# Low parts of the decay matrices on a second engine, and another bank order for the first FFN products

## The chip, the cores and the metric

The kernel runs on one core of a Trainium2 chip. Its metric is the device time of one execution in microseconds. A core has five engines with a program each: TensorE (PE), VectorE (DVE), ScalarE (ACT), GpSimd (POOL) and SyncE (SP), which here only issues DMAs. Each engine works through its program in order. They meet at semaphores: an instruction waits until a count is reached and raises another when it is done.

## The reference

```python
xn = layernorm(x)                                    # x: 2 x 2048 x 512
# one Mamba2 layer
x_branch, z = split(xn @ in_proj_w.T)                # 1024 columns each
x_branch = silu(causal_conv4(x_branch) + conv_b)
X, dt, B, C = split(x_branch @ x_proj_w.T)           # 16 heads of 64, state 128
dt = softplus(dt @ dt_proj_w.T + dt_proj_b);  A = -exp(A_log) * dt
L = exp(segsum(A))                                   # decay inside a chunk, lower triangle
Y = (C B^T * L) @ (X * dt) + C @ state * exp(cumsum(A))
Y = (Y + D * X) * silu(z);   attn = Y @ out_proj_w.T
# one ternary FFN
h = sigmoid(xn @ q(w1).T) * (xn @ q(w2).T);   ffn = h @ q(w3).T   # q: to -1, 0, 1
out = x + attn + ffn                                 # hidden size 1408
```

## The kernel before

The 4096 tokens are worked through in 8 blocks of 512 (256 of either sequence). A float32 operand is carried as two float16 tiles, a high part (a rounded copy) and a low part (what the rounding left), and a product is three matmuls: high by high, low by high, high by low.

One block has these stages. The branch products and the convolution come first (`x_branch`), then the projections to B, C and dt. Then come eight units u = 0..7, each one chunk of 128 tokens and one half of the heads. A unit holds:

- the decay matrices, in two groups g = 0, 1 of four heads (`decay`): ACT takes the differences of the running sums (L985) and their exponential (L990) into `edc[g]`, DVE multiplies by `gt`, the masked product of B and C (L1365), ACT writes the high part (L997) and DVE the low part (L1371) into one of four `mdc` tiles;
- the projection of X (PE L613), its copy to `xs` on ACT (L949), times dt on DVE (`xdt`, L1315), its high part on ACT (L955) and low part on DVE (L1319); POOL makes `xst` and the skip term from them (L1688, L1691);
- `scan`: PE multiplies decay matrices and `xdt` parts (L645, after a wait for `m_lo` and `xdt_lo`), DVE adds and gates (L1407, L1410); POOL adds the skip term to y before that (L1709);
- the state's update, the gate (`project_z`, PE L523, ACT L936, DVE L1262) and, for an earlier unit, the output projection (PE L696, from block 1 on) with its sum on DVE (L1433).

The decay matrices of unit u+1 are made while PE works on unit u. Then the FFN follows: 11 pairs of up products (PE L723, ACT L1032, DVE L1444) and the down products (L741), with the next block's branch products between them. The loops over blocks and units, written out for each engine, set the order of all instructions. A buffer or PSUM bank is taken again only after a wait for its last reader.

In block 0 the kernel also makes the ternary weights. Their thresholds come from sums over each matrix: PE adds them up in one column of bank 3 (L775), DVE turns this into bounds (L1466 to L1472), POOL compares (L1720) and DVE finishes the tile (L1487). Up product m, half j, goes to a bank that `up_bank` names:

```python
return banks[2 * ((m + 1) % 2) + j]
```

So up product 0 fills banks 2 and 3, and its second half, in bank 3, waits in block 0 until the third matrix's sum has been read there (`bounds` at 7). After up product 0 PE turns the last unit's y (L670, `turn_first(7)`), and after up product 1 it does the last output projection of block 0 (L680), which waits for the low part of that y (`yt_lo`, DVE L1421).

Of the kernel before, what the change touches and what calls it, by code (L numbers as in the profile page):

```python
# [8 lines left out]
ACT = mybir.ActivationFunctionType  # L9
# [5 lines left out]
P = 128  # L15
# [57 lines left out]
def mamba_ffn_block(nc, x, w_in, conv_w, conv_b, w_x, w_xdt, w_dt, dt_bias, a_log, d_skip, w_out,  # L73
# [48 lines left out]
    with ctx:  # L122
# [179 lines left out]
        def sync_program(sp):  # L302
# [12 lines left out]
            def load_prep(kind, n):  # L315
# [3 lines left out]
                if kind == "tern" and n >= n_early:  # L319
# [3 lines left out]
                    elif use >= 2:  # L323
                        sp.wait_ge(S["m_lo"], at(0, "m_lo", 12 + use))
# [145 lines left out]
        def tensor_program(pe):  # L470
# [163 lines left out]
            def scan(b, u):  # L634
# [4 lines left out]
                for g in range(2):  # L639
                    pe.wait_ge(S["m_lo"], at(b, "m_lo", 2 * u + g))  # L640
# [59 lines left out]
            def ffn_up(b, m):  # L700
                for j in range(2):
# [139 lines left out]
        def scalar_program(act):  # L841
# [11 lines left out]
            def x_branch(b, m):  # L853
# [119 lines left out]
            def decay(b, u):  # L973
                c, hf = units[u]
                for g in range(2):
# [3 lines left out]
                    if u:  # L979
                        act.wait_ge(S["m_lo"], at(b, "m_lo", 2 * (u - 1) + g))  # L980
# [10 lines left out]
                for g in range(2):  # L991
# [5 lines left out]
                    act.mul(mdc[2 * (u % 2) + g][:, 0, :], edc[g][:], M_SCALE / B_SCALE ** 2).then_inc(S["m_hi"], 1)  # L997
# [28 lines left out]
            def ffn_up(b, m):  # L1026
# [5 lines left out]
                act.activation(tnh[m % 2][:], up_bank(m, 0)[:], ACT.Tanh,  # L1032
# [129 lines left out]
        def vector_program(dve):  # L1162
# [196 lines left out]
            def decay(b, u):  # L1359
# [77 lines left out]
            def ffn_up(b, m):  # L1437
                dve.wait_ge(S["up_tanh"], at(b, "up_tanh", m))
                dve.wait_ge(S["up_mm"], at(b, "up_mm", 2 * m + 1))
                if b == 0 and m < 2:  # L1440
# [4 lines left out]
                                         in1=up_bank(m, 1)[:], op0=ALU.add,  # L1445
# [78 lines left out]
            for b in range(nb):  # L1524
# [33 lines left out]
                dve.tensor_tensor(gt[:], by_head(banks[3][:], P),  # L1558
# [257 lines left out]
```

## Time and profile before

| what | value |
|---|---|
| time, median of 3 runs | 1618.42 us (1616.63 to 1618.63) |
| the profiled execution's own time | 1617.01 us |
| its span, first to last instruction | 1615.2 us |
| PE busy | 1559.1 us, 97% |
| DVE, ACT, POOL busy | 1203.7, 886.9, 495.6 us |
| mean granted TensorE clock | 0.989 |

The span lies 1.8 us under the execution's own time, which holds the start and the end around it. Busy times of different engines overlap. PE's busy share is drawn with modelled ends of matmuls, so a short wait can hide under the end of the matmul before it. The DVE, ACT and POOL shares say how much they work, and not whether anyone waits for them.

### The profile page before, as it was taken

The page shows a single profiled execution, that of the slowest core. Times are in us where ns is not written, and L with a number is a line of the kernel's source. Part 1 is how long each engine was busy: PE and PEld are TensorE (multiplying, and loading weights), DVE is VectorE, ACT ScalarE, POOL GpSimd, SP SyncE. Part 2 cuts the span into 40 slices and gives each one's busy share as a digit, 9 for nine tenths or more (in the row PEclk, how much of TensorE's full clock was granted, in tenths as well). Part 3 has the DMA queues.
Part 4 walks back from the last instruction along what each step waited for, and adds up shares of the span by engine and source line. Part 5 has one row for each costly group of instructions (what it writes and reads, how often), then busy time and mean ns, then how long its engine had stood idle before and what let it go on. Part 6 is the DMA issues. An engine that isn't in the chain of part 4 may idle for free.

```text
span 1615.2 us, 25318 instructions
## 1 busy us (share of the span) xinstructions
PE 1559.1 (97%) x9086; PEld 744.3 (46%) x9086; DVE 1203.7 (75%) x1876; ACT 886.9 (55%) x1840; POOL 495.6 (31%) x480
## 2 busy tenths in 40 slices
PE   7779899999999999999999999999999999999999
PEld 3334444544444444444444444444444544444444
DVE  7878776699566985689856897568966699576862
ACT  6687435565356644466454663646636565356641
POOL 3116664233033321234221431314303233033210
PEclk9799999999999999999999999999999999999999
DMA  7155430242402432133321333213350242402320
GB/s 266 55 168 175 140 105 14 62 104 74 89 27 68 99 97 56 37 86 85 85 53 47 81 97 92 26 60 89 84 103 14 66 106 71 87 27 73 97 67 26
DMA packets 228605, 131.66 MB, mean 82 GB/s; under 512 B 175200, under 2 KB 176992, under 8 KB 228480
## 3 DMA queue, kind: packets, MB, share of 16 engines
q1 hardware_dynamic: 228480, 130.05, 30.0%
q8 instruction: 72, 1.18, 0.3%
q14 instruction: 53, 0.43, 0.1%
HBM read 100.38 MB, written 29.62 MB: 80 GB/s over the span
## 4 chain that ended last, share of the span: by engine, by line
PE 62%; DVE 18%; issue 7%; ACT 5%; DMA 2%; POOL 2%; SPq 1%; DVEq 0%; POOLq 0%; ACTq 0%
PE bank L723 12%; PE bank L613 11%; PE bank L741 9%; PE bank L507 9%; PE bank L523 6%; PE bank L533 4%; DVE edc L1365 4%; PE bank L696 4%; DVE xst_lo L1336 2%; ACT edc L985 2%; PE bank L645 1%; DVE xin L1407 1%; DVE xdt L1315 1%; ACT mdc L997 1%; DVE xs L1414 1%
## 5 line engine op out<-in xcount | busy, mean ns | idle before, releaser
L613 PE MATMUL bank<-wx_hi,arena 128*128 128x512 f16 x1024 | 319.7, 382 | 0.0
L723 PE MATMUL bank<-xt_hi,q 128*128 128x512 f16 x704 | 267.0, 379 | 4.0 <-issue 4.0
L723 PE MATMUL bank<-xt_lo,q 128*128 128x512 f16 x704 | 267.0, 379 | 0.0
L1688 POOL TENSOR_TENSOR xst<-xdt,dst 128x512 f32<-128x512 f32 x60 | 62.6, 1043 | 490.3 <-DVE xdt L1315 490.3
L613 PE MATMUL bank<-wx_lo,arena 128*128 128x512 f16 x512 | 195.9, 383 | 0.0
L741 PE MATMUL bank<-q,arena 128*128 128x512 fp8e4 x704 | 163.3, 381 | 0.0
L985 ACT ACTIVATE edc<-csl,csv 128x128 f32<-128x128 f32 x512 | 155.8, 389 | 0.8 <-DMA csl<-sums 0.8
L1365 DVE TENSOR_TENSOR edc<-edc,gt 128x512 f32<-128x512 f32 x128 | 125.9, 1022 | 38.7 <-ACT edc L990 38.6
L613 PEld LDWEIGHTS bank<-wx_hi,arena 128*128 128x128 f16 x1024 | 101.1, 99 | 114.7 <-issue 3.7
L1024 ACT CAST arena<-full 128x512 f16<-128x512 f32 x88 | 54.2, 616 | 146.4 <-DVE full L1444 146.4
L1709 POOL TENSOR_TENSOR xin<-xin,xs 128x512 f32<-128x512 f32 x60 | 83.8, 1397 | 153.0 <-DVE xin L1388 153.0
L997 ACT ACTIVATE mdc<-edc 128x512 f16<-128x512 f32 x128 | 79.4, 630 | 61.5 <-DVE edc L1365 61.5
L723 PEld LDWEIGHTS bank<-xt_hi,q 128*128 128x128 fp8e4 x704 | 69.1, 98 | 87.7 <-issue 4.7
L741 PEld LDWEIGHTS bank<-q,arena 128*128 128x128 f16 x704 | 69.1, 98 | 83.6 <-issue 1.1
L723 PEld LDWEIGHTS bank<-xt_lo,q 128*128 128x128 fp8e4 x704 | 68.9, 98 | 82.8 <-issue 0.3
L955 ACT ACTIVATE xdt_hi<-xdt 128x512 f16<-128x512 f32 x64 | 40.3, 630 | 120.4 <-DVE xdt L1315 120.4
L507 PE MATMUL bank<-xt_hi,win_hi 128*128 128x512 f16 x256 | 97.0, 379 | 3.2 <-DVE win_lo L1229 2.5
L1691 POOL TENSOR_TENSOR xs<-xs,dsk 128x512 f32<-128x512 f32 x64 | 93.7, 1464 | 18.5 <-DVE xdt L1315 18.5
L1444 DVE SCALAR_TENSOR_TENSOR full<-tnh,bank 128x512 f32<-128x512 f32 x88 | 60.0, 682 | 52.0 <-PE bank L723 50.4
L523 PE MATMUL bank<-win_hi,xt_hi 128*128 128x512 f16 x256 | 97.1, 379 | 0.8 <-DVE xin L1262 0.7
L523 PE MATMUL bank<-win_lo,xt_hi 128*128 128x512 f16 x256 | 97.0, 379 | 0.0
L523 PE MATMUL bank<-win_hi,xt_lo 128*128 128x512 f16 x256 | 97.0, 379 | 0.0
(217 smaller groups left out, 3419.2 us busy)
## 6 DMA issues: line engine op xcount, KB each, us to landing
csl<-sums SPq DMA_DIRECT2D x128, 256.0 KB, 3.6
y_squares<-xs SPq DMA_DIRECT2D x56, 256.0 KB, 2.0
xin<-y_squares SPq DMA_DIRECT2D x168, 64.0 KB, 2.5
xin<-x SPq DMA_DIRECT2D x32, 256.0 KB, 4.0
res<-x SPq DMA_DIRECT2D x32, 256.0 KB, 3.4
out<-res SPq DMA_DIRECT2D x32, 256.0 KB, 2.0
raw<-w_ffn SPq DMA_DIRECT2D x25, 256.0 KB, 2.9
x_squares<-mdc SPq DMA_DIRECT2D x24, 256.0 KB, 2.0
```

Source lines behind the costliest of these rows:

```text
L507: i = pe.matmul(bk[:], wt[:, k, m * P:(m + 1) * P], act[:, k, :], start=(n == 1), stop=(n == 3 * kd))
L523: i = pe.matmul(banks[1][:], act[:, k, c * P:(c + 1) * P], wt[:, k, di + hf * half:di + (hf + 1) * half], start=(n == 1), stop=(n == 3 * kd))
L533: i = pe.matmul(bk[:], wt[:, k, col:col + ns], act[:, k, :], start=(n == 1), stop=(n == 3 * ki))
L613: i = pe.matmul(banks[0][:], act[:, k, c * P:(c + 1) * P], wt[:, k, hf * half:(hf + 1) * half], start=(n == 1), stop=(n == 3 * ki))
L696: i = pe.matmul(banks[7][:], act[:, k, :], wt[:, k, :], start=(hf == 0 and n == 1), stop=(hf == 1 and n == 3 * per))
L723: i = pe.matmul(up_bank(m, j)[:], q12[:, j, m, k, :], part[:, k, :], start=(n == 1), stop=(n == 2 * kd))
L741: i = pe.matmul(banks[c][:], hid[:, m, p, c * P:(c + 1) * P], q3[:, m, :], start=(m == p == 0), stop=(m == kf - 1 and p == 1))
L985: i = act.activation(edc[g][:, cols], csl[g][:, cols], ACT.Relu, scale=-1.0, bias=sml["csv"][:, c, h:h + 1])
L997: act.mul(mdc[2 * (u % 2) + g][:, 0, :], edc[g][:], M_SCALE / B_SCALE ** 2).then_inc(S["m_hi"], 1)
L1365: dve.tensor_tensor(by_head(edc[g][:], P), by_head(edc[g][:], P), gt[:, c, :].unsqueeze(1).to_broadcast([P, hpg, P]), ALU.mult).then_inc(S ...
L1691: pool.tensor_tensor(by_head(xs[u % 2][:], hd), by_head(xs[u % 2][:], hd), heads_over(dsk[:], hf * hph, hph, hd), ALU.mult).then_inc(S["sk ...
L1709: pool.tensor_tensor(yac[u % 2][:], yac[u % 2][:], xs[u % 2][:], ALU.add).then_inc(S["y_skip"], 1)
```

## The change

There are two parts. From block 1 on, POOL writes the low part of group g = 1 of each unit with a tensor_tensor, ahead of `project_x` in its program; DVE keeps group 0, and both groups in block 0. For that the scale (a power of two) moves from L997 and L1371 into `gt`, and the semaphore `m_lo` becomes `m_lo0` and `m_lo1`. In block 0 alone, up product m takes banks 0 and 1 for even m and 2 and 3 for odd m, the reverse of before; the waits on the banks go with them, and so do those of the down products.

```diff
-        def up_bank(m, j):
-            return banks[2 * ((m + 1) % 2) + j]
+        def up_bank(b, m, j):
+            return banks[2 * ((m + (b > 0)) % 2) + j]
...
-                    elif m == 0 and j == 0:
+                    elif m == (0 if b else 1) and j == 0:
                         pe.wait_ge(S["btok"], at(b, "btok", 0))
-                    elif m == 0:
+                    elif m == (0 if b else 1):
                         pe.wait_ge(S["gt"], at(b, "gt", 0))
                         if b == 0:
                             pe.wait_ge(S["bounds"], 7)
                     elif j == 0:
                         pe.wait_ge(S["xs"], at(b, "xs", 7))
...
+                        last = 9 + c // 2 if b else 10 - c // 2
                         if m == 0 and c % 2 == 0:
-                            pe.wait_ge(S["up_tanh"], at(b, "up_tanh", 9 + c // 2))
+                            pe.wait_ge(S["up_tanh"], at(b, "up_tanh", last))
...
-                    pe.wait_ge(S["m_lo"], at(b, "m_lo", 2 * u + g))
+                    pe.wait_ge(S[f"m_lo{g}"], at(b, f"m_lo{g}", u))
...
-                    act.mul(mdc[2 * (u % 2) + g][:, 0, :], edc[g][:], M_SCALE / B_SCALE ** 2).then_inc(S["m_hi"], 1)
+                    act.copy(mdc[2 * (u % 2) + g][:, 0, :], edc[g][:]).then_inc(S["m_hi"], 1)
...
-                for g in range(2):
+                for g in range(2 if b == 0 else 1):
                     md = mdc[2 * (u % 2) + g]
                     dve.wait_ge(S["m_hi"], at(b, "m_hi", 2 * u + g))
-                    dve.scalar_tensor_tensor(out=md[:, 1, :], in0=edc[g][:], scalar=M_SCALE / B_SCALE ** 2,
-                                             in1=md[:, 0, :], op0=ALU.mult,
-                                             op1=ALU.subtract).then_inc(S["m_lo"], 1)
+                    dve.scalar_tensor_tensor(out=md[:, 1, :], in0=edc[g][:], scalar=1.0, in1=md[:, 0, :],
+                                             op0=ALU.mult, op1=ALU.subtract).then_inc(S[f"m_lo{g}"], 1)
...
-                dve.tensor_tensor(gt[:], by_head(banks[3][:], P),
-                                  upp[:].unsqueeze(1).to_broadcast([P, chunks, P]),
-                                  ALU.mult).then_inc(S["gt"], 1)
+                dve.scalar_tensor_tensor(out=gt[:], in0=by_head(banks[3][:], P), scalar=M_SCALE / B_SCALE ** 2,
+                                         in1=upp[:].unsqueeze(1).to_broadcast([P, chunks, P]),
+                                         op0=ALU.mult, op1=ALU.mult).then_inc(S["gt"], 1)
...
+            def decay(b, u):
+                md = mdc[2 * (u % 2) + 1]
+                pool.wait_ge(S["m_hi"], at(b, "m_hi", 2 * u + 1))
+                pool.tensor_tensor(md[:, 1, :], edc[1][:], md[:, 0, :],
+                                   ALU.subtract).then_inc(S["m_lo1"], 1)
...
+                if b:
+                    decay(b, 0)
                 project_x(b, 0)
...
                     if u + 1 < len(units):
+                        if b:
+                            decay(b, u + 1)
                         project_x(b, u + 1)
```

On PE, between unit 7 of block 0 and its last output projection, the order was this (names in brackets are the semaphores waited for; `bank2` is PSUM bank 2, `q12` the ternary weights of the up products):

```order
L775 MATMUL bank3<-tsum,ones 128x1 [waits mag_sum,bounds,gt]
L723 MATMUL bank2<-xt_hi,q12 128x512 [waits tern_q,btok]
...
L723 MATMUL bank3<-xt_hi,q12 128x512 [waits tern_q,bounds,gt]
...
L670 MATMUL bank7<-idn,xin 128x128 [waits y_gated,yt_lo]
...
L723 MATMUL bank0<-xt_hi,q12 128x512 [waits tern_q,xs]
...
L723 MATMUL bank1<-xt_hi,q12 128x512 [waits tern_q,gate]
...
L680 MATMUL bank7<-wo_hi,yt_hi 128x512 [waits yt_lo]
```

In the changed kernel the same stretch of PE reads so:

```order
L778 MATMUL bank3<-tsum,ones 128x1 [waits mag_sum,bounds,gt]
L724 MATMUL bank0<-xt_hi,q12 128x512 [waits tern_q,xs]
...
L724 MATMUL bank1<-xt_hi,q12 128x512 [waits tern_q,gate]
...
L671 MATMUL bank7<-idn,xin 128x128 [waits y_gated,yt_lo]
...
L724 MATMUL bank2<-xt_hi,q12 128x512 [waits tern_q,btok]
...
L724 MATMUL bank3<-xt_hi,q12 128x512 [waits tern_q,bounds,gt]
...
L681 MATMUL bank7<-wo_hi,yt_hi 128x512 [waits yt_lo]
```

The wait for `bounds` has moved from the second to the fourth of these products, behind the transposes.

On DVE the units 0 and 1 of every block from 1 on began like this, from the first decay matrices on:

```order
L1365 TENSOR_TENSOR edc<-edc,gt 128x512 x2
L1371 SCALAR_TENSOR_TENSOR mdc<-edc,mdc 128x512 x2
L1315 TENSOR_TENSOR xdt<-xs,dt 128x512
L1319 SCALAR_TENSOR_TENSOR xdt_lo<-xdt,xdt_hi 128x512
L1336 SCALAR_TENSOR_TENSOR xst_lo<-xst,xst_hi 128x512
L1388 SCALAR_TENSOR_TENSOR xin<-bank,ecs 128x512
L1365 TENSOR_TENSOR edc<-edc,gt 128x512 x2
L1371 SCALAR_TENSOR_TENSOR mdc<-edc,mdc 128x512 x2
L1262 SCALAR_TENSOR_TENSOR xin<-tnh,bank 128x512
L1407 SCALAR_TENSOR_TENSOR xin<-bank,xin 128x512
L1410 TENSOR_TENSOR xin<-xin 128x512
L1315 TENSOR_TENSOR xdt<-xs,dt 128x512
```

In the changed kernel the same place on DVE is:

```order
L1368 TENSOR_TENSOR edc<-edc,gt 128x512 x2
L1375 SCALAR_TENSOR_TENSOR mdc<-edc,mdc 128x512
L1318 TENSOR_TENSOR xdt<-xs,dt 128x512
L1322 SCALAR_TENSOR_TENSOR xdt_lo<-xdt,xdt_hi 128x512
L1339 SCALAR_TENSOR_TENSOR xst_lo<-xst,xst_hi 128x512
L1391 SCALAR_TENSOR_TENSOR xin<-bank,ecs 128x512
L1368 TENSOR_TENSOR edc<-edc,gt 128x512 x2
L1375 SCALAR_TENSOR_TENSOR mdc<-edc,mdc 128x512
L1265 SCALAR_TENSOR_TENSOR xin<-tnh,bank 128x512
L1410 SCALAR_TENSOR_TENSOR xin<-bank,xin 128x512
L1413 TENSOR_TENSOR xin<-xin 128x512
L1318 TENSOR_TENSOR xdt<-xs,dt 128x512
```

One of each pair of low parts is gone. On POOL a unit of the changed kernel reads so, with the new instruction third:

```order
L1712 TENSOR_TENSOR state<-state,dec 128x512
L1719 TENSOR_TENSOR xin<-xin,xs 128x512
L1701 TENSOR_TENSOR mdc<-edc,mdc 128x512
L1691 TENSOR_TENSOR xst<-xdt,dst 128x512
L1694 TENSOR_TENSOR xs<-xs,dsk 128x512
```

It stands between the sum of y and the skip term and the product that makes `xst`; nothing else moved there.

## Rows read from the trace of the kernel before

**Rows 1.** The page: the span, and busy time by engine.
```profile
span 1615.2 us, 25318 instructions
PE 1559.1 (97%) x9086; PEld 744.3 (46%) x9086; DVE 1203.7 (75%) x1876; ACT 886.9 (55%) x1840; POOL 495.6 (31%) x480
```

**Rows 2.** Busy time by stage: window, length, then each engine, clock, DMA; block 4.
```profile
1019.00:1213.00 194.00, 192.29 (x1131) 91.19 (x1129) 146.97 (x230) 106.24 (x219) 56.17 (x57) 1.00 0.29 72
```

**Rows 3.** Whom PE waited for, whole run: us in total, times, longest.
```profile
PE bank L696 <- DVE res L1433: 6.1, 6, 1.6
PE bank L723 <- issue: 4.0, 1, 4.0
```

**Rows 4.** Timeline of block 0's FFN (start, us, engine, line); last row: the chain's.
```profile
188.95 0.38 PE L723 MATMUL bank<-xt_lo,q 128*128 128x512 f16 x1
193.04 0.15 DVE L1466 TENSOR_SCALAR gam<-bank 128x1 f32<-128x1 f32 x1
193.29 0.38 PE L723 MATMUL bank<-xt_hi,q 128*128 128x512 f16 x1 [3.96 <-issue]
193.36 0.74 DVE L1487 SCALAR_TENSOR_TENSOR q<-full,above,less 128x512 fp8e4<-128x512 f32 x1
198.91 0.38 PE L680 MATMUL bank<-wo_hi,yt_hi 128*128 128x512 f16 x1
207.81 0.69 DVE L1444 SCALAR_TENSOR_TENSOR full<-tnh,bank 128x512 f32<-128x512 f32 x1 [1.44 <-PE bank L723]
238.40 2.44 PE L486 MATMUL bank<-idn,xin 128*128 128x128 f32 x13 [2.09 <-DVE xin L1179]
...
405.40 13.81 PE bank L723 x64
```

**Rows 5.** Timeline of block 4, units 0 and 1.
```profile
1077.90 1.23 ACT L997 ACTIVATE mdc<-edc 128x512 f16<-128x512 f32 x2 [0.24 <-DVE edc L1365]
1078.56 1.29 DVE L1371 SCALAR_TENSOR_TENSOR mdc<-edc,mdc 128x512 f16<-128x512 f32 x2
1079.04 0.58 ACT L949 ACTIVATE xs<-bank 128x512 f32<-128x512 f32 x1
1079.77 0.68 DVE L1315 TENSOR_TENSOR xdt<-xs,dt 128x512 f32<-128x512 f32 x1
1080.54 1.04 POOL L1688 TENSOR_TENSOR xst<-xdt,dst 128x512 f32<-128x512 f32 x1 [30.83 <-DVE xdt L1315]
1081.15 0.97 DVE L1319 SCALAR_TENSOR_TENSOR xdt_lo<-xdt,xdt_hi 128x512 f16<-128x512 f32 x1 [0.70 <-ACT xdt_hi L955]
1082.18 0.20 PE L645 MATMUL bank<-xdt_hi,mdc 128*128 128x64 f16 x1
1087.43 0.58 ACT L936 ACTIVATE tnh<-bank 128x512 f32<-128x512 f32 x1
1088.16 0.68 DVE L1262 SCALAR_TENSOR_TENSOR xin<-tnh,bank 128x512 f32<-128x512 f32 x1
1088.90 0.39 PE L523 MATMUL bank<-win_hi,xt_hi 128*128 128x512 f16 x1
```

**Rows 6.** Timeline of block 4, decay of unit 7, and PE behind its scan.
```profile
1161.38 1.47 DVE L1371 SCALAR_TENSOR_TENSOR mdc<-edc,mdc 128x512 f16<-128x512 f32 x2
1161.49 0.63 ACT L997 ACTIVATE mdc<-edc 128x512 f16<-128x512 f32 x1 [1.05 <-DVE edc L1365]
1163.48 0.69 DVE L1410 TENSOR_TENSOR xin<-xin 128x512 f32<-128x512 f32 x1
1164.09 0.68 DVE L1315 TENSOR_TENSOR xdt<-xs,dt 128x512 f32<-128x512 f32 x1
1176.86 0.39 PE L696 MATMUL bank<-wo_hi,yt_hi 128*128 128x512 f16 x1 [0.91 <-DVE res L1433]
```

**Rows 7.** POOL forms: two in the timeline, one group (us busy, mean ns).
```profile
1109.10 1.27 POOL L1709 TENSOR_TENSOR xin<-xin,xs 128x512 f32<-128x512 f32 x1 [3.03 <-DVE xin L1388]
1159.26 1.65 POOL L1709 TENSOR_TENSOR xin<-xin,xs 128x512 f32<-128x512 f32 x1 [3.63 <-DVE xin L1388]
...
L1720 POOL TENSOR_SCALAR less<-raw,under 128x512 uint8<-128x512 f32 x14 | 25.4, 1820 | 8.0 <-DMA raw<-w_ffn 4.6 <-DVE q L1487 3.4
```

More of the change, by code:

```diff
@@ L42 @@
               "silu": 8, "s_lo": 8, "gate": 8, "dt_step": 19, "cs_rest": 2, "bt_lo": 1, "ct_lo": 1, "xst_lo": 8, "st_lo": 8, "gt": 1,
-              "xdt": 8, "xdt_lo": 8, "m_mult": 16, "m_lo": 16, "yoff": 8, "y_added": 8, "state": 8,
+              "xdt": 8, "xdt_lo": 8, "m_mult": 16, "m_lo0": 8, "yoff": 8, "y_added": 8, "state": 8,
               "y_gated": 8, "y_blocks": 8, "yt_lo": 8, "attn": 4, "hid_f": 11, "hid_lo": 11, "out_ready": 4}
 POOL_EVENTS = {"rstd_pow": 1, "halo_in": 8, "halo_out": 8, "convadd": 8, "skip": 8, "xe": 8,
-               "sd": 8, "y_skip": 8}
+               "sd": 8, "y_skip": 8, "m_lo1": 8}
 ONCE = ("y_turned", "first_out", "cleared", "win_hi", "win_lo", "z_hi", "z_lo", "bc_hi", "bc_lo", "wx_hi", "wx_lo",
@@ L323, in load_prep @@
                     elif use >= 2:
-                        sp.wait_ge(S["m_lo"], at(0, "m_lo", 12 + use))
+                        sp.wait_ge(S[f"m_lo{use - 2}"], at(0, f"m_lo{use - 2}", 7))
                     else:
@@ L722, in ffn_up @@
                             n += 1
-                            i = pe.matmul(up_bank(m, j)[:], q12[:, j, m, k, :],
+                            i = pe.matmul(up_bank(b, m, j)[:], q12[:, j, m, k, :],
                                           part[:, k, :], start=(n == 1), stop=(n == 2 * kd))
@@ L731, in ffn_down @@
                         between(c, m)
+                        last = 9 + c // 2 if b else 10 - c // 2
                         if m == 0 and c % 2 == 0:
-                            pe.wait_ge(S["up_tanh"], at(b, "up_tanh", 9 + c // 2))
+                            pe.wait_ge(S["up_tanh"], at(b, "up_tanh", last))
                         elif m == 0:
-                            pe.wait_ge(S["hid_f"], at(b, "hid_f", 9 + c // 2))
+                            pe.wait_ge(S["hid_f"], at(b, "hid_f", last))
                         if c == 0:
@@ L870, in x_branch @@
                     if m < 2:
-                        act.wait_ge(S["m_lo"], at(b - 1, "m_lo", 14 + m))
+                        act.wait_ge(S[f"m_lo{m}"], at(b - 1, f"m_lo{m}", 7))
                     elif m < 4:
@@ L979, in decay @@
                     if u:
-                        act.wait_ge(S["m_lo"], at(b, "m_lo", 2 * (u - 1) + g))
+                        act.wait_ge(S[f"m_lo{g}"], at(b, f"m_lo{g}", u - 1))
                     elif g:
@@ L1031, in ffn_up @@
                     act.wait_ge(S["gate"], at(b, "gate", 6 + m))
-                act.activation(tnh[m % 2][:], up_bank(m, 0)[:], ACT.Tanh,
+                act.activation(tnh[m % 2][:], up_bank(b, m, 0)[:], ACT.Tanh,
                                scale=0.5 / XN_SCALE).then_inc(S["up_tanh"], 1)
@@ L1444, in ffn_up @@
                 dve.scalar_tensor_tensor(out=full[m % 2][:], in0=tnh[m % 2][:], scalar=1.0,
[L1445 removed]
+                                         in1=up_bank(b, m, 1)[:], op0=ALU.add,
                                          op1=ALU.mult).then_inc(S["hid_f"], 1)
```

## The prediction

> **What bounds the kernel now.** I read the page's busy times first. PE is busy for 1559.1 us of a span of 1615.2 us [rows 1]. The stages came next: block 4 has PE busy for 192.29 of 194.00 us at full clock, and DVE for 146.97 us [rows 2]. So PE sets the pace, and work taken off DVE is worth only what PE waits for DVE. The list of PE's waits shows where. The wait of L696 for DVE's L1433 comes six times and costs 6.1 us. In block 0 there is one wait of 4.0 us at L723, put down to "issue" [rows 3]. Last I read the timeline at these places, because an idle figure under-reports here. A matmul of 512 columns is drawn 0.38 us long, but 64 of them start in 13.81 us, 0.216 us apart [rows 4]. A true wait is therefore idle time plus about 0.16 us.
>
> **Block 0, the banks.** PE starts the last matmul of the first product at 188.95 and the next product only at 193.29 [rows 4]. DVE's read of the third sum (L1466) runs from 193.04 to 193.19, so the wait is the one for `bounds`, not for weights. In the new order the second half of up product 0 goes to bank 1, which was free long ago, and starts at 189.17. Eight matmuls (1.73 us) bring PE to 190.9. Four small transposes and the first half of product 1 (1.73 us) are over before 193.29 if the transposes take less than 0.66 us, and I take that they do. The second half of product 1 waits for the same L1466, until 193.29, and ends at 195.02. L680 then needs the low part of the last y on DVE: L1487 from 193.36, L1444 0.66 us on, L1421 0.60 us later and 0.69 us long, so 195.31. L680 starts at about 195.36 and not at 198.91: **3.55 us** earlier.
>
> Is this given back in the FFN? PE next waits for the normalised x at 238.40 (2.09 us), behind a long chain of DVE and POOL [rows 4]. That chain hangs on PE at its start: DVE is idle for 1.44 us before 207.81, waiting for the third up product. The weights of the second loop step wait for the same DVE position, and so do the loads behind them. So the whole stage moves with PE, and I count all 3.55 us. If the chain were held by something fixed in time, all of it would be gone.
>
> **From block 1 on, what is removed.** DVE loses 56 L1371 of 0.60 to 0.69 us each [rows 5], some 35 us. Almost all of it lies beside PE's work and is worth nothing. Three places per block can matter: the scan of unit 0 (PE at 1082.18), the gate of unit 1 (PE at 1088.90) and the wait of L696 at 1176.86 [rows 5, 6]. ACT's copy instead of its scaled copy, and the scale inside `gt`, have the same sizes and forms as before: nothing.
>
> **What is added.** POOL gets one tensor_tensor per unit, reading float32 and float16, writing float16. The trace has no such form. The nearest row is L1709, two full float32 inputs, 1.27 us [rows 7]. The lower end is L1688, with one input repeated within a head, 1.04 us [rows 5]; the upper end is L1720, which writes a narrower type than it reads, 1.82 us [rows 7]. I take P = 1.27 us.
>
> The duration matters because of who shares what. DVE's L1319 starts at 1081.15, while POOL's L1688 runs until 1081.58, and takes 0.97 us instead of the 0.69 us of its like: it ends 0.54 us after POOL does. POOL's L1709 takes 1.65 us instead of 1.27 when it meets DVE's L1365 [rows 5, 7]. So a DVE instruction with both inputs in SBUF and a POOL tensor_tensor do not run together; the later one waits, and DVE ends about 0.55 us after POOL. The Trainium skill, "SBUF — State Buffer", section "Who interferes with whom", has this as a rule: a DVE instruction with two SBUF inputs and a GpSimd instruction that reads SBUF want the same port, and the first one holds it to its end. The trace agrees (0.97 us), and by this rule the new POOL work can put DVE back.
>
> *Unit 0.* ACT ends the second high part at 1079.13 and POOL starts at 1079.20. ACT ends `xs` at 1079.62, and DVE's L1315 (inputs `xs` and `dt`, both SBUF) finds POOL running until 1080.47. It ends at 1081.02, where it ended at 1080.45 before: 0.57 us late. L1319 behind it is late by as much (1082.12 before), and PE at 1082.18 starts right behind it and is as late. *Unit 1.* L1262 no longer stands behind a second L1371 but behind ACT's tanh, which ends at 1088.01; it gains 0.12 us, so PE's 1088.90 comes 0.45 us late. The scan of unit 1 waits for DVE too and keeps the 0.45. In units 2 to 6 PE's list has no wait for `xdt_lo` or the gate. Cost: 7 blocks by 0.45 = **3.15 us**.
>
> *Unit 6.* DVE's L1407 reads PSUM and goes on. POOL runs from ACT's 1162.12 + 0.06 to 1163.45; L1410 (two SBUF inputs) waits for it and ends at 1164.00 instead of 1164.17. So L1315 starts 0.17 us earlier, of the 0.61 us that the removed instruction took. DVE is behind ACT there already, so the same gain of the unit before is carried in: 0.35 us in all. The line of DVE work up to L1433 moves with it, and the wait of 0.91 + 0.16 us at L696 shrinks by 0.35 us, in the 6 blocks that have it [rows 3, 6]: **-2.1 us**.
>
> Sum: -3.55 + 3.15 - 2.1 = **-2.5 us**. Against the profiled execution's 1617.01 us this is 1614.5 us. The median of the runs shown lies 1.41 us above that execution, so I put the new median at **1615.9 us**.
>
> As a function of P the cost per block is P - 0.82 and the gain at L696 about twice 1.44 - P. With P = 1.04: -3.55 + 1.54 - 4.8 = -6.8 us. With P = 1.82: -3.55 + 7.0 + 4.6 = +8 us. The Trainium skill, "GPSIMD Engine Reference", section "3.1 Elementwise — side-by-side cycle accounting", gives 2.6 cycles per element for two inputs; at that page's 1.2 GHz, 512 elements would be an estimated 1.11 us before the fixed part. By that page alone the sum would be -5.5 us. The L1709 row at 1.27 us is the measured one.
>
> **Rivals.**
> 1. *The two engines do not block each other with this float16 form.* Then unit 0 loses nothing, L1315 gains 0.11 us and the gate 0.12 us per block (7 by 0.12 = 0.8 us), and the wait at L696 is gone (0.61 us per unit, carried; 6 by 1.07 = 6.4 us). With block 0: -10.8 us, 1607.6 us. For it: L1407 and L1262 run beside POOL untouched. Against it: the stretched L1319 and L1709 [rows 5, 7].
> 2. *POOL's float16 form is slow, and the decay of unit 0 becomes PE's wait.* Place: L1315 of unit 0 behind the new POOL instruction. It decides against the change from P = 1.40 us on; at P = 1.6 it gives -3.55 + 5.5 + 1.9 = +3.8 us, 1622.2 us. For it: L1720 with another output type, 1.82 us. Against it: three forms of tensor_tensor lie at 1.04 to 1.27 us.
> 3. *Block 0 gives its gain back* at the normalisation before 238.40: +1.0 us, 1619.5 us. Against it: DVE's idle time before 207.81.
> 4. *P near 1.04 us*, since a float16 input is half the bytes: 1611.6 us.
>
> **How the numbers follow.** Forecast 0.42, rival 4 0.22, rival 2 0.17, rival 1 0.10, rival 3 0.09. A measurement of this kernel tells about 0.2%, 3.2 us, from no change: faster is below 1615.2 us, slower above 1621.7 us. The forecast's own range is 1613.5 to 1618 us, so a third of it (0.15) and rivals 1 and 4 count as faster: 0.47. Slower is most of rival 2: 0.15. The rest, 0.38, is no change. The range reaches from rival 1 to rival 2, 1607.5 to 1621.5 us.
>
> **What would show it.** In the profile after: no wait of 4 us at the up products of block 0, and the output projection behind up product 1 starts near 195.4; a new DVE L1315 of 1.3 us or more in unit 0 of blocks 1 to 7, with the new POOL instruction beside it; L645 of unit 0 later by about 0.6 us, counted from the block's start; the waits at L696 0.5 to 0.8 us instead of 0.91. Blocks 1 to 6 should take 193.5 us, as before, within 0.3 us. I am wrong if the blocks from 1 on change by over 0.5 us each, if the POOL instruction is not between 1.1 and 1.4 us, or if PE still stands at 238 us in block 0.

## The result, and the profile after

The changed kernel takes 1608.57 us (median of 4 runs, 1608.44 to 1609.1), the kernel before 1618.53 us in the runs beside it. The medians lie 10.0 us apart. The ratio is 0.9948, 95% interval 0.9936 to 0.9959: 0.5% faster, about 8.4 us, with 6.6 to 10.4 us inside the interval. The forecast was 1615.9 us. The time lies in the forecast range, near its lower end: the gain is three to four times the forecast one. One execution of the kernel before, beside e5 to e8, took 1821.34 us at a granted clock of 0.848 and is left out of all ratios and spreads here.

The profiled execution took 1608.5 us, 1606.4 of it span. The busy times of the page answer to [rows 1]:

```profile
span 1606.4 us, 25318 instructions
PE 1556.3 (97%) x9086; PEld 743.1 (46%) x9086; DVE 1173.1 (73%) x1820; ACT 888.1 (55%) x1840; POOL 550.7 (34%) x536
```

DVE lost 56 instructions and 30.6 us, POOL got 56 and 55 us. Where the time went is seen by the stage. PE's first branch product of a block (L507 before, L508 now) is a mark that every block has. Both kernels, blocks counted from 0:

```
block                           0       1       2       3       4       5       6       7
before, us                 243.71  195.29  193.57  193.50  193.81  193.47  193.34  208.54
after, us                  238.60  194.81  193.05  192.60  193.26  192.61  192.59  208.86
after - before              -5.11   -0.48   -0.52   -0.90   -0.55   -0.86   -0.75   +0.32
```

These are differences of the marks (the first column is the time up to the start of block 1). So block 0 gives 5.1 us, blocks 1 to 6 give 4.1 us, and the last block loses 0.3 us: the 8.85 us of the two spans. (The stretch that the prediction calls block 4, near 1019.88 to 1213.35 us, is block 5 in this count: the branch products that open it are issued inside the down products of the block ahead.)

PE's list of waits, which answers to [rows 3] (engine, tensor and line, what it waited for: us in all, times, longest):

```profile
PE bank L646 <- issue: 7.2, 11, 2.2
PE bank L646 <- DVE xdt_lo L1322: 4.3, 8, 0.9
PE bank L697 <- DVE res L1436: 0.8, 1, 0.8
```

The 4.0 us at the up products are gone, and so are five of the six waits of the output projection (L697) for DVE; the sixth, in block 1, is 0.8 us long.

**Block 0**, the timeline that answers to [rows 4] (start us, us, engine, line, operation, tiles, idle before):

```profile
187.61 0.59 PE L724 MATMUL bank<-xt_hi,q 128*128 128x512 f16 x1
...
191.83 0.60 PE L671 MATMUL bank<-idn,xin 128*128 128x128 f32 x4
...
193.06 0.15 DVE L1469 TENSOR_SCALAR gam<-bank 128x1 f32<-128x1 f32 x1
...
194.93 0.68 DVE L1424 SCALAR_TENSOR_TENSOR yt_lo<-bank,yt_hi 128x512 f16<-128x512 f32 x1
...
195.72 0.38 PE L681 MATMUL bank<-wo_hi,yt_hi 128*128 128x512 f16 x1
...
234.96 1.64 PE L487 MATMUL bank<-idn,xin 128*128 128x128 f32 x13 [2.08 <-DVE xin L1182]
```

PE runs through both up products while DVE's read of the third sum (L1469) still ends at 193.21, at the same place as before. L681 starts at 195.72 instead of 198.91, and the wait for the normalised x ends at 234.96 instead of 238.40, still 2.08 us long. The stage has moved with PE.

**Unit 0 of block 5**, which answers to [rows 5]; L1318, L1375, L1322, L952 and L1000 are L1315, L1371, L1319, L949 and L997 of before:

```profile
1070.33 1.22 ACT L1000 CAST mdc<-edc 128x512 f16<-128x512 f32 x2 [0.24 <-DVE edc L1368]
1070.98 0.69 DVE L1375 SCALAR_TENSOR_TENSOR mdc<-edc,mdc 128x512 f16<-128x512 f32 x1
1071.46 0.59 ACT L952 ACTIVATE xs<-bank 128x512 f32<-128x512 f32 x1
1071.63 1.16 POOL L1701 TENSOR_TENSOR mdc<-edc,mdc 128x512 f16<-128x512 f32 x1 [29.50 <-ACT mdc L1000]
1072.08 1.25 DVE L1318 TENSOR_TENSOR xdt<-xs,dt 128x512 f32<-128x512 f32 x1 [0.41 <-ACT xs L952]
1075.06 0.20 PE L646 MATMUL bank<-xdt_hi,mdc 128*128 128x64 f16 x1 [0.49 <-DVE xdt_lo L1322]
```

POOL's new instruction ends at 1072.79, and DVE's L1318, drawn 1.25 us long where its like takes 0.68, ends 0.54 us after it.

**Unit 7 and the output projection**, which answer to [rows 6]:

```profile
1151.49 1.94 DVE L1368 TENSOR_TENSOR edc<-edc,gt 128x512 f32<-128x512 f32 x2 [0.56 <-ACT edc L993]
...
1154.16 1.16 POOL L1701 TENSOR_TENSOR mdc<-edc,mdc 128x512 f16<-128x512 f32 x1 [1.88 <-ACT mdc L1000]
1154.84 1.03 DVE L1413 TENSOR_TENSOR xin<-xin 128x512 f32<-128x512 f32 x1
1155.79 0.68 DVE L1318 TENSOR_TENSOR xdt<-xs,dt 128x512 f32<-128x512 f32 x1
...
1157.17 0.97 DVE L1322 SCALAR_TENSOR_TENSOR xdt_lo<-xdt,xdt_hi 128x512 f16<-128x512 f32 x1 [0.70 <-ACT xdt_hi L958]
...
1161.16 0.19 PE L646 MATMUL bank<-xdt_hi,mdc 128*128 128x64 f16 x1
...
1167.82 0.68 DVE L1436 SCALAR_TENSOR_TENSOR res<-bank,res 128x512 f32<-128x512 f32 x1
```

The reader is to see three things. DVE's L1413 is held by POOL (1.03 us instead of 0.69, end 0.55 us after POOL's). DVE now waits 0.56 us for ACT at L1368, where before it did not wait: it is no longer behind ACT at this place. And `xdt_lo` is ready at 1158.14, 3.02 us ahead of PE's scan at 1161.16. Before it was less:

```profile
1165.46 0.97 DVE L1319 SCALAR_TENSOR_TENSOR xdt_lo<-xdt,xdt_hi 128x512 f16<-128x512 f32 x1 [0.69 <-ACT xdt_hi L955]
...
1168.39 0.19 PE L645 MATMUL bank<-xdt_hi,mdc 128*128 128x64 f16 x1
```

1168.39 - 1166.43 = 1.96 us. Call this difference DVE's lead over PE. Worked out so for every unit of block 5, it is the key of what follows:

```
unit                        0     1     2     3     4     5     6     7
lead before, us          0.06  0.10  1.58  1.60  1.62  1.27  1.45  1.96
lead after, us           0.06  0.10  1.87  2.16  2.46  2.16  2.46  3.02
gain                     0     0     0.29  0.56  0.84  0.89  1.01  1.06
```

### The profile page after: what moved, and what is told of

Same layout as the page of the kernel before. It is cut to its first block, busy times and chain, and to the rows that moved or that the text cites. A ratio compares the mean times of both kernels' runs of the same rounds, so it can differ in the third digit from the quotient of the medians.

```text
span 1606.4 us, 25318 instructions
## 1 busy us (share of the span) xinstructions
PE 1556.3 (97%) x9086; PEld 743.1 (46%) x9086; DVE 1173.1 (73%) x1820; ACT 888.1 (55%) x1840; POOL 550.7 (34%) x536
## 4 chain that ended last, share of the span: by engine, by line
PE 78%; DVE 7%; issue 4%; ACT 4%; DMA 2%; POOL 2%; SPq 1%; POOLq 0%; DVEq 0%; ACTq 0%
PE bank L614 16%; PE bank L724 13%; PE bank L508 9%; PE bank L744 9%; PE bank L524 8%; PE bank L697 8%; PE bank L534 5%; PE bank L646 3%; PE bank L658 2%; PE bank L631 2%; ACT edc L988 2%; POOL less L1730 1%; DMA xin<-x_squares 1%; PE bank L561 1%; DVE edc L1368 1%
## 5 line engine op out<-in xcount | busy, mean ns | idle before, releaser
L1701 POOL TENSOR_TENSOR mdc<-edc,mdc 128x512 f16<-128x512 f32 x56 | 64.8, 1156 | 299.8 <-ACT mdc L1000 299.8
L1368 DVE TENSOR_TENSOR edc<-edc,gt 128x512 f32<-128x512 f32 x128 | 110.5, 902 | 56.7 <-ACT edc L993 56.6
L1719 POOL TENSOR_TENSOR xin<-xin,xs 128x512 f32<-128x512 f32 x60 | 76.7, 1278 | 154.4 <-DVE xin L1391 154.4
L1000 ACT CAST mdc<-edc 128x512 f16<-128x512 f32 x128 | 78.1, 618 | 43.4 <-DVE edc L1368 43.4
L508 PE MATMUL bank<-xt_hi,win_hi 128*128 128x512 f16 x256 | 98.0, 383 | 2.8 <-DVE win_lo L1232 1.8
L1678 POOL COPY hal<-raw 128x6 f32<-128x6 f32 x64 | 29.0, 453 | 208.4 <-ACT raw L866 208.2
L508 PE MATMUL bank<-xt_lo,win_hi 128*128 128x512 f16 x256 | 98.0, 383 | 0.0
L508 PE MATMUL bank<-xt_hi,win_lo 128*128 128x512 f16 x256 | 97.8, 382 | 0.0
L524 PE MATMUL bank<-win_hi,xt_hi 128*128 128x512 f16 x256 | 97.1, 379 | 0.7 <-DVE xin L1265 0.7
```

The source lines that it names most:

```text
L508: i = pe.matmul(bk[:], wt[:, k, m * P:(m + 1) * P], act[:, k, :], start=(n == 1), stop=(n == 3 * kd))
L524: i = pe.matmul(banks[1][:], act[:, k, c * P:(c + 1) * P], wt[:, k, di + hf * half:di + (hf + 1) * half], start=(n == 1), stop=(n == 3 * kd))
L1000: act.copy(mdc[2 * (u % 2) + g][:, 0, :], edc[g][:]).then_inc(S["m_hi"], 1)
L1368: dve.tensor_tensor(by_head(edc[g][:], P), by_head(edc[g][:], P), gt[:, c, :].unsqueeze(1).to_broadcast([P, hpg, P]), ALU.mult).then_inc(S ...
L1701: pool.tensor_tensor(md[:, 1, :], edc[1][:], md[:, 0, :], ALU.subtract).then_inc(S["m_lo1"], 1)
L1719: pool.tensor_tensor(yac[u % 2][:], yac[u % 2][:], xs[u % 2][:], ALU.add).then_inc(S["y_skip"], 1)
```

## The experiments

Two theories stood after the first look. **Carry**: each unit leaves DVE 1.44 - P earlier (the prediction's own term, with P = 1.16 us as measured), 0.28 us, and all of it is handed to the next unit, so that the waits at L697 go entirely. **Port**: POOL's two-input instruction and a DVE instruction with both inputs in SBUF exclude each other, which costs 0.44 us in unit 0 of each block and is where a faster version is to be found. Their rivals: the gain at L697 comes from the last unit alone, or from the moved scale; and L1318 is long for a reason other than POOL. The new bank order is a question by itself. Kernels in one group below ran on one chip beside the same runs of the kernel before.

**The parts apart: e1, e2, e3, e4** (before beside them: 1617.86 us).

e1 is the kernel before with the bank order of block 0 alone:

```diff
-            return banks[2 * ((m + 1) % 2) + j]
+            return banks[2 * ((m + (b > 0)) % 2) + j]
```

(the waits on the banks go with it, as in the change)

> The kernel before with the other bank order in block 0 alone; DVE keeps all low parts. Theory A (the banks take away the wait of 4 us at the up products and the FFN stage moves with PE): 3.2 to 5.2 us faster than before, about 1614.5 us, the upper figure if TensorE's clock also stays up behind the x transposes. Theory B (the gain is given back at the wait for the normalised x): within 1 us of before.

Measured: 1612.87 us, ratio 0.9970 (0.9959 to 0.9981), so -5.0 us. The wait at the up products is gone, and the waits at the output projection of the later blocks stand as in [rows 3]:

```profile
PE bank L696 <- DVE res L1434: 6.1, 6, 1.5
```

e2 is the changed kernel with the banks of before:

```diff
-            return banks[2 * ((m + (b > 0)) % 2) + j]
+            return banks[2 * ((m + 1) % 2) + j]
```

(again with the waits that belong to them)

> The changed kernel with the bank order of before: POOL makes the low parts of group 1 from block 1 on. Theory A (DVE's lead over PE grows unit by unit, so the wait at L697 goes in six blocks, 6 by 1.07 us, and unit 0 costs 7 by 0.33 to 0.44 us): 3.4 to 4.1 us faster than before, about 1614.6 us. Theory of the prediction (only two units' worth of gain, 2.1 us, against 3.15 us of cost): 1.0 us slower, 1619.5 us.

Measured: 1612.09 us, ratio 0.9965 (0.9951 to 0.9978), so -5.8 us. The list of waits again has the one of block 0:

```profile
PE bank L724 <- issue: 4.0, 1, 4.0
```

-5.0 and -5.8 make -10.8 us, against -10.0 by the medians and -8.4 by the ratio with both: within the intervals (about 2 us each) the two parts add.

e3 keeps the scale in `gt` and ACT's plain copy, and gives both low parts back to DVE:

```diff
-                for g in range(2 if b == 0 else 1):
+                for g in range(2 if True else 1):
...
-                if b:
-                    decay(b, 0)
...
-                        if b:
-                            decay(b, u + 1)
```

(with the banks of before)

> The kernel before with the scale moved into gt and ACT's high part as a plain copy; DVE makes both low parts, the banks are those of before. Both theories: nothing, within 1 us of 1618.5 us. If it is faster by over 1 us, ACT's copy or the form of L1371 has a part in the gain.

Measured: 1617.6 us, ratio 0.9994 (0.9983 to 1.0005). The moved scale is worth nothing that the runs can tell (the interval is 1.8 us to either side), and the waits at the output projection are there, six of them:

```profile
PE bank L697 <- DVE res L1436: 5.4, 6, 0.9
```

So the gain from block 1 on comes from POOL's share alone.

e4 leaves unit 0 of every block to DVE (POOL from unit 1 on):

```diff
-                for g in range(2 if b == 0 else 1):
+                for g in range(2 if b == 0 or u < 1 else 1):
...
-                if b:
-                    decay(b, 0)
```

> The changed kernel, but unit 0 of each block has both low parts on DVE. Theory A (in unit 0 L1318 waits for the POOL instruction to end, which makes the scan of unit 0 0.44 us late and the gate of unit 1 0.33 us): 7 by about 0.3 us faster than the changed kernel, 2.1 us, about 1606.5 us; L1318 of unit 0 takes 0.68 us and the scan of unit 0 comes 62.3 us after the block's start instead of 62.7. Rival (the lateness of unit 0 does not reach the block's end): within 0.5 us of 1608.6 us.

Measured: 1606.1 us, ratio 0.9927 (0.9914 to 0.9939); again as **e12** below. The timeline of its unit 0:

```profile
1070.80 1.29 DVE L1375 SCALAR_TENSOR_TENSOR mdc<-edc,mdc 128x512 f16<-128x512 f32 x2
1072.01 0.68 DVE L1318 TENSOR_TENSOR xdt<-xs,dt 128x512 f32<-128x512 f32 x1
...
1074.42 0.20 PE L646 MATMUL bank<-xdt_hi,mdc 128*128 128x64 f16 x1
```

L1318 takes 0.68 us again, and PE's first scan comes 62.29 us after the block's start (1012.13), as before (62.30), and not 62.74 us after it. The lead at unit 7 is 3.00 us all the same: unit 0 of a block gives nothing to the later ones, because PE waits for DVE there anyway and the lead starts again at 0.06 us.

**Carry: e5 and e6** (before beside them and e7, e8: 1617.19 us). e5 has POOL in unit 7 alone, e6 from unit 2 on; the edit is that of e4, with 7 and with 2:

```diff
+                for g in range(2 if b == 0 or u < 7 else 1):
...
-                        if b:
+                        if b and u + 1 >= 7:
```

> The changed kernel, but POOL makes the low part of unit 7 alone in each block from 1 on; units 0 to 6 have both on DVE. Carry theory (each unit's decay gives DVE about 0.28 us, and the gains of units 2 to 7 add up to over the 1.07 us that PE waited at L697): here only 0.28 us of it goes, the wait at L697 stays at about 0.6 us of idle time, and the total is 2 to 3 us over the changed kernel, about 1611.0 us, with the scan of unit 0 at 62.3 us. Rival (the last unit's own instruction decides the wait): the wait is gone and the total is about 1606.5 us, as with unit 0 alone kept on DVE.

Measured: 1609.67 us, ratio 0.9957 (0.9944 to 0.9970). Its lead at unit 7:

```profile
1158.52 0.97 DVE L1322 SCALAR_TENSOR_TENSOR xdt_lo<-xdt,xdt_hi 128x512 f16<-128x512 f32 x1 [0.69 <-ACT xdt_hi L958]
...
1161.73 0.19 PE L646 MATMUL bank<-xdt_hi,mdc 128*128 128x64 f16 x1
```

1161.73 - 1159.49 = 2.24 us, 0.28 more than before, where the changed kernel has 1.06 more; and all six waits at the output projection stay, 0.6 us long at most (PE's waits over the whole run, where the changed kernel has one of L697):

```profile
PE bank L697 <- DVE res L1436: 3.8, 6, 0.6
```

Both are what carry says. Block 5 takes 193.06 us, between 193.47 and 192.61. The time as a whole is 1.3 us better than carry's figure; with intervals of about 2 us this alone could not decide, the lead does.

> The changed kernel with both low parts on DVE in units 0 and 1. Carry theory: units 2 to 7 are enough for L697; against the version with unit 0 alone on DVE the gate of unit 1 comes 0.12 us later in 7 blocks: about 1606.9 us. Rival (unit 1 counts for more): over 1608 us.

Measured: 1605.76 us, ratio 0.9934 (0.9919 to 0.9948). Lead 2.99 us at unit 7, block 5 in 192.29 us. Unit 1 adds nothing to the later units either: PE waits for DVE there, and the lead is 0.10 us in every one of these kernels. Leaving unit 1 to DVE costs a little all the same. PE's scan of unit 1 comes 72.64 us after the block's start here and 72.54 us in e4, and block 5 takes 192.29 us against e4's 192.19.

**Port: e7, e8, e9.** e7 puts a memset in the place of POOL's subtraction, so the low parts of group 1 are left out of the product:

```diff
-                pool.tensor_tensor(md[:, 1, :], edc[1][:], md[:, 0, :],
-                                   ALU.subtract).then_inc(S["m_lo1"], 1)
+                pool.memset(md[:, 1, :], 0.0).then_inc(S["m_lo1"], 1)
```

> The changed kernel with a memset in place of POOL's subtraction, so the low parts of group 1 are left out from block 1 on; POOL then reads nothing from SBUF there. Port theory (a POOL instruction that reads SBUF keeps a DVE instruction with two SBUF inputs waiting): L1318 of unit 0 takes 0.68 us again and L1413 0.69 us, the scan of unit 0 comes 62.2 us after the block's start and the gate of unit 1 gains too; 3 to 4 us under the changed kernel, about 1605 us. Rival (the waits of L1318 and L1413 are for something else, as the later start of DVE's work): L1318 stays at 1.2 us or the total at 1608.6 us.

Measured: 1603.49 us, ratio 0.9921 (0.9907 to 0.9935).

```profile
1068.57 0.53 POOL L1701 MEMSET mdc<- 128x512 f16 x1 [29.48 <-ACT mdc L1000]
1069.04 0.69 DVE L1318 TENSOR_TENSOR xdt<-xs,dt 128x512 f32<-128x512 f32 x1 [0.41 <-ACT xs L952]
```

L1318 starts 0.06 us before the memset ends and takes 0.69 us; the first scan comes at 62.19 us in the block. L1318 is no longer than elsewhere. The overlap is so short, though, that this does not show that a memset leaves DVE alone: L1318 ends 0.63 us after the memset, and would look the same if it had been held until 0.55 us after it. What e7 shows is that POOL's subtraction, by its length or by what it reads, is what holds L1318 in the changed kernel. The lead grows to 3.67 us at unit 7 (1157.56 - 1153.89). The whole kernel is 1.5 us under the figure expected: POOL's 0.53 us are shorter than 1.16 everywhere, and L1413 is not held either.

e8 doubles the suspect: two more POOL subtractions of half the width ahead of each of the 56, into tiles that nothing needs then:

```diff
+                pool.wait_ge(S["m_lo1"], at(b, "m_lo1", u - 1))
+                pool.wait_ge(S["tern_q"], n_ff)
+                for t in less:
+                    pool.tensor_tensor(t[:].bitcast(F16), edc[1][:, 0:half // 2], md[:, 0, 0:half // 2],
+                                       ALU.subtract)
```

> The changed kernel, with two more POOL subtractions of half the width (into tiles that nothing reads) ahead of each low part, so POOL holds on about 1.3 us longer per unit; POOL's busy share stays under 45%. Port theory: L1318 of unit 0 ends 1.3 us later (7 by 1.3 = 9 us), L1413 ends later than before the change in each unit, so DVE falls behind PE from unit 3 on: 15 to 50 us over the changed kernel. Rival (POOL has slack, and DVE's loss in unit 0 is an accident of one place): within 2 us of 1608.6 us.

Measured: 1648.98 us, ratio 1.0200 (1.0184 to 1.0217), +31.8 us against before, some 40 us against the changed kernel.

```profile
1118.96 1.30 POOL L1704 TENSOR_TENSOR less<-edc,mdc 128x256 f16<-128x256 f32 x2 [1.88 <-ACT mdc L1000]
1119.64 1.17 DVE L1413 TENSOR_TENSOR xin<-xin 128x512 f32<-128x512 f32 x1
1120.22 1.60 POOL L1706 TENSOR_TENSOR mdc<-edc,mdc 128x512 f16<-128x512 f32 x1
1120.73 1.64 DVE L1318 TENSOR_TENSOR xdt<-xs,dt 128x512 f32<-128x512 f32 x1
```

Here the two engines take turns, and each is held in its turn: L1413 takes 1.17 us until after POOL's pair ends at 1120.26; L1706, issued meanwhile, takes 1.60 instead of 1.16 us; and L1318 behind it takes 1.64 us and ends 0.55 us after L1706. In unit 0 the expectation missed. There L1318 meets only the first of POOL's half-width instructions, takes 0.76 us and ends earlier than in the changed kernel; it is L1322 that is held (1.49 instead of 0.97 us), and the first scan comes at 62.78 us in the block, not 1.3 us after 62.74. The loss shows from unit 1 on, whose scan comes at 74.53 instead of 72.99 us. The lead is eaten: PE now waits at the gate (L524), at the scan and at the output projection (waits from 640 us on):

```profile
PE bank L524 <- DVE xin L1265: 4.6, 5, 0.9
PE bank L697 <- DVE res L1436: 4.4, 4, 1.1
PE bank L658 <- DVE xst_lo L1339: 2.9, 4, 0.7
```

Block 5 takes 199.02 us. That is 6.4 us more per block than the changed kernel for work on an engine that is idle for more than half the span.

e9 asks whether a POOL instruction with one input blocks too. It copies the full decay in place of the difference, so the low parts hold other values:

```diff
+                pool.tensor_copy(md[:, 1, :], edc[1][:]).then_inc(S["m_lo1"], 1)
```

> The changed kernel with a tensor_copy of edc in place of POOL's subtraction, so the low parts of group 1 are wrong from block 1 on; POOL reads one SBUF operand and not two. If any POOL read of SBUF keeps a DVE instruction with two SBUF inputs waiting: L1318 of unit 0 ends 0.55 us after POOL's copy does, and takes more than 0.68 us where the copy is still running at its start. If only POOL instructions with two inputs do: L1318 takes 0.68 us beside a running copy. In both cases the total lies between the version with the memset and the changed kernel, 1603.5 to 1608.6 us.

Measured (before beside it: 1616.70 us): 1603.79 us, ratio 0.9919 (0.9906 to 0.9933).

```profile
1069.38 0.61 POOL L1701 CAST mdc<-edc 128x512 f16<-128x512 f32 x1 [29.49 <-ACT mdc L1000]
1069.85 0.69 DVE L1318 TENSOR_TENSOR xdt<-xs,dt 128x512 f32<-128x512 f32 x1 [0.41 <-ACT xs L952]
```

This doesn't decide. The copy is so short that it ends 0.14 us into L1318, and L1318 ends 0.69 us after its own start and 0.55 us after the copy's end: both readings give the same picture. The kernel before has a longer one-input instruction on POOL, the comparison L1720 of block 0, with a two-input DVE instruction (L1410) wholly inside it:

```profile
187.27 2.00 POOL L1720 TENSOR_SCALAR less<-q,under 128x512 uint8<-128x512 f32 x1
188.47 0.69 DVE L1410 TENSOR_TENSOR xin<-xin 128x512 f32<-128x512 f32 x1
```

DVE is not held there. It is POOL's instruction that is longer than the 1.56 us which the same form takes at 148.22 us. So not every POOL instruction that reads SBUF holds DVE to its end; which forms do stays open.

**Repeats: e10, e11, e12**, on one chip with e9: e6's kernel, the changed kernel and e4's kernel again.

> The version with POOL's low parts in units 2 to 7 alone, timed again beside the changed kernel: 1605.8 us, 2 to 3 us under the changed kernel. If the difference was chance, both lie within 1 us.

> The changed kernel itself, timed again on the chip of the other two: 1608.6 us, 8 to 10 us under the kernel before.

> The version with POOL's low parts in units 1 to 7, timed again: within 1 us of the version from unit 2 on; by theory 0.1 us per block faster (the gate of unit 1), so 0.7 us, which this can hardly tell.

Measured: e10 1605.39 us (0.9931, 0.9919 to 0.9944); e11 1608.07 us (0.9944, 0.9930 to 0.9958; five runs, 1606.96 to 1609.32); e12 1604.98 us (0.9927, 0.9915 to 0.9940; five runs, 1603.8 to 1606.05). No run of e12 is as slow as any of e11. The 3.1 us between them are seven blocks by 0.44 us, which is what unit 0 of a block gives back. This version, POOL's share without unit 0, beats both kernels; e6's is as good within the intervals, 0.1 us per block behind by the traces.

## Why the prediction came out as it did

*PE sets the pace; DVE's time is worth only what PE waits for it.* Right: DVE lost 30.6 us, and PE's gain from block 1 on is 3.7 us.

*Block 0, 3.55 us.* Right in mechanism, 0.36 us too much at L681: 195.72 instead of 195.36. PE's own work and DVE's low part (ready at 195.61) were late by about as much: the second product ended 0.7 us later than I had counted, at 195.7. In this execution PE's first matmuls from 187.61 on are 0.42 us apart instead of 0.216, at a reduced clock (0.69 of full from 183 to 193 us). *Is it given back?* No: the move at L487 is 3.44 us. Rival 3 is false.

*Block 0, another 1.7 us that no step had, and that were luck.* Between L487 and the start of block 1 the same PE work takes 5.30 us before and 3.64 us after. The windows (us, then busy time and count of PE, PEld, DVE, ACT, POOL, granted clock, DMA), first of before, then of after:

```profile
238.40:243.70 5.30, 5.30 (x23) 3.40 (x24) 5.14 (x9) 2.76 (x5) 1.94 (x2) 0.68 0.00 0
```

```profile
234.96:238.60 3.64, 3.64 (x24) 2.40 (x25) 3.64 (x7) 2.56 (x5) 1.89 (x1) 1.00 0.00 0
```

At 0.68, an estimated 3.4 of the 5.3 us ran at the lower of the clock's two levels, 1.2 GHz, which costs 1.7 us. Ahead of both stretches PE had waited 2.1 us. Is this the change's doing? The other traces say no. In e11, the changed kernel itself in another execution, the same stretch reads:

```profile
233.79:239.10 5.31, 5.31 (x24) 3.60 (x25) 4.99 (x9) 2.86 (x5) 1.88 (x1) 0.68 0.00 0
```

It takes 5.27 to 5.32 us in e4, e6 to e10 and e12 too, all with the new banks, and 3.63 us in e2 and e3, which have the old ones. In e2 the dip stands elsewhere, behind the 4.0 us wait that is back there (window from 193 to 198 us):

```profile
193.00:198.00 5.00, 5.00 (x20) 2.61 (x19) 1.98 (x3) 1.70 (x3) 2.89 (x2) 0.71 0.91 291
```

So a fair comparison takes in both places. From the transposes near 184 us to the start of block 1, PE takes 59.9 us in all three kernels with the old banks, 56.4 to 57.0 us in eight of the eleven with the new ones, and 54.8 to 55.5 us in the other three: the changed kernel's first profile, e1 and e5. The new order is thus worth 2.9 to 3.5 us, as forecast, and the rest came in three executions of eleven. e1's -5.0 us, with an interval of 1.8 us to either side, can't tell 3.4 from 5.1.

*The scale inside `gt` and ACT's copy: nothing.* Right (e3, 0.9994).

*P = 1.27 us.* The new instruction takes 1.156 us in the mean of 56, between the lower end (1.04) and the value taken:

```profile
L1701 POOL TENSOR_TENSOR mdc<-edc,mdc 128x512 f16<-128x512 f32 x56 | 64.8, 1156 | 299.8 <-ACT mdc L1000 299.8
```

With this P, the prediction's own formula gives P - 0.82 = 0.34 us of cost in a block, a gain of 0.57 us at each L696, and in all -4.6 us, 1613.8 us. So the wrong P is the smaller part of the miss. The estimate of 1.11 us before a fixed part, worked out from the Trainium skill, "GPSIMD Engine Reference", section "3.1 Elementwise — side-by-side cycle accounting", lies nearer to the measured value than the row of L1709 that I took.

*Unit 0 and unit 1: 0.57 us late at the scan, 0.45 after the gate, 3.15 us in all.* The mechanism is right. The first scan comes 0.44 us later in the block (62.30 to 62.74) and the second 0.33 us later (72.66 to 72.99), each 0.12 to 0.13 us less than forecast, which is the 0.11 us of P. (L1318 takes 1.25 us, where the forecast had named 1.3 or more.) e4 and e12 take this cost away, and e8 makes it 1.87 us at the scan of unit 1. The rule of the Trainium skill that the prediction weighed ("SBUF — State Buffer", section "Who interferes with whom") holds here: DVE's two-input instruction ends 0.54 to 0.55 us after POOL's tensor_tensor in all of these rows; for a POOL instruction with one input the row of L1720 above does not agree. Rival 1 denied the blocking; its figure, 1607.6 us, lies nearest to the measured time, but its mechanism is false. It had the wait at L696 gone, which is right, and a gain where units 0 and 1 in truth cost 2.3 us; luck in block 0 and the spread of the runs made up for that.

*Unit 6 and L696: "the same gain of the unit before is carried in: 0.35 us in all", -2.1 us.* This is the step that failed, and it is the term of the sum that was mis-sized. I let two units' gains reach L696, on the ground that DVE is behind ACT there. The runs show that every unit from 2 on adds its own: 0.29, 0.56, 0.84 us in units 2 to 4. Yet DVE waits for ACT at L1368 in these units, before (0.50, 0.29 and 0.31 us) and after (0.50, 0.57 and 0.86 us), and ACT's part comes at a time that PE sets. So being behind ACT is not what hands the gain on. POOL's sum for y does. DVE's L1391 starts it, and it holds the L1368 that follows. Unit 4's decay in block 5, before and then after:

```profile
1121.44 1.26 POOL L1709 TENSOR_TENSOR xin<-xin,xs 128x512 f32<-128x512 f32 x1 [3.03 <-DVE xin L1388]
1121.67 2.19 DVE L1365 TENSOR_TENSOR edc<-edc,gt 128x512 f32<-128x512 f32 x2 [0.31 <-ACT edc L990]
```

```profile
1113.64 1.27 POOL L1719 TENSOR_TENSOR xin<-xin,xs 128x512 f32<-128x512 f32 x1 [3.03 <-DVE xin L1391]
1114.43 1.63 DVE L1368 TENSOR_TENSOR edc<-edc,gt 128x512 f32<-128x512 f32 x2 [0.86 <-ACT edc L993]
```

After the change DVE's pair starts 0.56 us later against POOL's instruction, and still it ends 1.15 us after it, as before (1.16). So what DVE saves by L1391 is saved at the end of L1368 too. The prediction knew this hold (L1709 of 1.65 us) and did not follow it from unit to unit. That the hold of L1719 is the path is read from the traces; no run took it away alone.

From unit 5 on less is added (0.05 to 0.12 us per unit). There the first L1365 ran ahead of L1709 before the change, and now both stand behind it, which takes about 0.2 us. The gain is bounded as well: in e7, with 0.61 us per unit, the lead has grown by 1.51 us at unit 4 and by 1.71 us at unit 7, since L1368 there waits up to 1.48 us for ACT and is then not held at all. In the changed kernel the gain is 1.06 us by L697, as much as the wait had (0.91 + 0.16 us [rows 3, 6]), so the wait is gone. Over the six blocks 6.1 us of idle time became 0.8, and with 0.16 us for each of the five waits that went this is 6.1 us instead of 2.1. e5 shows it from the other side: with one unit's share on POOL the lead gains 0.28 us and all six waits stay. In the last block there is no such wait at stake and the cost stands alone: +0.32 us, as the formula has it (0.34).

Put together again, with the sizes that the traces show: -3.4 by order and -1.7 by clock in block 0, 7 by 0.33 = +2.3 in units 0 and 1, -6.1 at the output projection, in all -8.9 us against the 8.85 us between the spans. Without the luck of the clock it is -7.2 us. Of the 6.4 us between this and the forecast -2.5, the output projection has 4.0, the clock 1.7 and units 0 and 1 have 0.9; block 0's order gave 0.15 less than forecast. The single blocks scatter about this: 0.5 us in blocks 1, 2 and 4, 0.8 to 0.9 in 3, 5 and 6, of which only block 1's is accounted for, by the wait that is left.

The forecast of the blocks, "193.5 us, as before, within 0.3 us", was therefore wrong in five of the six (192.6 us in three), and the sign that I had named for being wrong, "over 0.5 us each", came true in those five. P and block 0 were in their bounds. That the total fell inside the range owes something to its width: the lower end was rival 1's figure. (Its upper end, 1621.5 us, was said to reach rival 2, whose figure is 1622.2.)

## What to carry to other kernels

Follow a saving per unit from one unit to the next before comparing it with the wait at the end. It is handed on as long as what ends the next step hangs on the engine that saved, directly or through another (here POOL's sum, which DVE starts and which holds DVE's next product). It stops being handed on where PE waits for that engine, or where a feeder that does not depend on it comes last. Here six units of 0.28 us made 1.06 us, not 0.28 and not 1.68. Moving elementwise work to POOL helps where DVE's time is carried on to a wait of PE, and hurts where POOL's new instruction meets a two-input one of DVE's that PE waits for. Sort the units of a loop by that, and leave out those that lose (here unit 0, worth 3.1 us of 1605; unit 1, where the new instruction holds nothing that PE waits for, is better by 0.1 us with it). And when the time of a rival fits, look for its mechanism in the trace before believing it.

## What the runs showed of the hardware

- POOL's two-input subtraction of 512 columns, float32 and float16 to float16, takes 1.156 us, less than with two full float32 inputs (1.28 us, L1719 in the mean) and more than with one input repeated within a head (1.04 us). Half the columns take 0.67 us where nothing holds them, more than half the time, and 0.78 us in the mean with those that DVE held (1.11 us); a copy to float16 takes 0.61 us and a memset 0.53 us:

```profile
L1704 POOL TENSOR_TENSOR less<-edc,mdc 128x256 f16<-128x256 f32 x112 | 84.5, 776 | 288.1 <-ACT mdc L1000 288.1
```

```profile
L1701 POOL CAST mdc<-edc 128x512 f16<-128x512 f32 x56 | 34.1, 609 | 302.6 <-ACT mdc L1000 302.6
```

- Where DVE's two-input instruction finds POOL's tensor_tensor running, it ends 0.54 to 0.55 us after POOL's, and not its full 0.68 us after; in e8 POOL is held by DVE as well (1.60 instead of 1.16 us).
- The stretch at a reduced clock after a wait of PE comes at another place, or is missing, in profiles of nearly the same kernel (0.68 at 238.4 us before, 0.71 at 193 us in e2), and even of the same one (1.00 at 235 us after, 0.68 at 234 us in e11). Single executions of the kernel before spread over 1614.8 to 1620.8 us, more than most of the terms argued here.
